# Feed-forward stages in turns of two batches, and later sends to the experts' slots, in a one-core transformer kernel

## The reference

```python
x = x + 0.5 * ffn(LN(x))       # 128 -> 512 -> 128, gelu, signs of w1 and a scale per row
x = x + gated_attention(LN(x)) # groups of 32 rows, a quadratic and a linear part
x = x + 0.5 * ffn(LN(x))       # the same weights once more
x = x + 0.5 * moe(LN(x))       # 8 experts, top 2, at most 76 rows per expert and batch, silu(h * g)
x = x + linear_attention(LN(x))# 16 heads, elu + 1
x = x + 0.5 * moe(LN(x))       # the same weights once more
```

## Time and profile before

| what | value |
|---|---|
| median of three runs | 2290.44 us (2286.01 to 2292.85) |
| profiled execution | 2287.4 us |
| its span on the core | 2285.4 us |
| mean granted TensorE clock | 0.987 of full |
| TensorE matmul busy | 2177.7 us, 95% |
| VectorE busy | 1520.7 us, 67% |
| ScalarE busy | 1241.2 us, 54% |
| GpSimd busy | 685.5 us, 30% |

### The profile page before, as it was taken

One profiled execution on the slowest core, in us unless ns is written; L12 is line 12 of the kernel. 1 busy time (PEld: TensorE's weight loads), 2 busy tenths in 40 slices (PEclk: granted clock), 3 DMA queues, 4 the chain that ended last, 5 costly groups with the idle time before them and its releaser, 6 DMA issues. The chain is left out here.

```text
span 2285.4 us, 42519 instructions
## 1 busy us (share of the span) xinstructions
PE 2177.7 (95%) x13706; PEld 1753.3 (77%) x13706; DVE 1520.7 (67%) x4922; ACT 1241.2 (54%) x2504; POOL 685.5 (30%) x724
## 2 busy tenths in 40 slices
PE   5989998999999999899999999999999899999995
PEld 5978888977777777777677777877777777777775
DVE  6867776866677776556666566666666676777664
ACT  4645445655444554465566665666665444544542
POOL 0412222433575555500000000000100344665545
PEclk9999999999999999999999999999999999999998
DMA  8040000000111111200000000000000011111222
GB/s 275 0 175 0 0 0 1 2 10 23 35 42 41 37 38 47 54 5 0 0 0 0 0 0 1 1 1 1 1 1 1 12 28 40 45 51 50 51 54 73
DMA packets 70648, 68.44 MB, mean 30 GB/s; under 512 B 9312, under 2 KB 57952, under 8 KB 70112
## 3 DMA queue, kind: packets, MB, share of 16 engines
q1 hardware_dynamic: 60960, 47.62, 6.5%
q0 software_dynamic: 8192, 16.79, 3.2%
q10 hardware_dynamic: 1344, 2.16, 0.3%
HBM read 32.47 MB, written 34.08 MB: 29 GB/s over the span
## 5 line engine op out<-in xcount | busy, mean ns | idle before, releaser
L2031 ACT ACTIVATE moe_fc<-moe_bank,all_b_fc 128x380 f32<-128x380 f32 (+2 forms) x448 | 245.8, 549 | 301.4 <-PE moe_bank L1961 298.3
L2138 DVE SCALAR_TENSOR_TENSOR moe_act<-moe_bank,all_b_moe_gate,moe_fc 128x380 f32<-128x380 f32 (+2 forms) x448 | 256.9, 576 | 169.5 <-PE moe_bank L1965 107.1
L1977 PEld LDWEIGHTS moe_bank<-all_w_proj,moe_act 128*128 128x128 f32 x2560 | 300.0, 192 | 12.2 <-issue 2.4
L1977 PE MATMUL moe_bank<-all_w_proj,moe_act 128*128 128x128 f32 x2560 | 305.7, 276 | 2.0 <-DVE moe_expert_out L2147 2.0
L1800 POOL DMA_INDIRECT all_landed<-rows_out,all_take_at x256 | 267.5, 1045 | 117.8 <-issue 114.5
L1494 POOL COPY lin_xn_ones<-lin_xn 128x254 f32<-128x254 f32 x32 | 12.7, 398 | 722.8 <-PE lin_bank L1244 722.4
L1876 POOL TENSOR_SCALAR moe_hot<-all_slot_ids,moe_slot 128x608 fp32r<-128x608 f32 x112 | 202.3, 1814 | 67.6 <-DVE moe_slot L2115 32.8
L2038 ACT ACTIVATE moe_act<-moe_act 128x760 f32<-128x760 f32 (+2 forms) x224 | 174.8, 780 | 85.0 <-DVE moe_act L2138 84.3
L1388 ACT ACTIVATE lin_neg<-lin_bank 128x512 f32<-128x512 f32 x256 | 151.7, 593 | 105.8 <-PE lin_bank L1236 62.1
L1286 PEld LDWEIGHTS lin_bank<-lin_kv,lin_qT 128*128 128x128 f32 x1024 | 145.1, 192 | 74.3 <-issue 62.3
L1961 PE MATMUL moe_bank<-gau_rowsT,all_w_fc 128*128 128x380 f32 (+2 forms) x448 | 171.4, 464 | 1.6 <-ACTq L2042 1.6
(11 more groups left out here) (248 smaller groups left out, 4557.0 us busy)
## 6 DMA issues: line engine op xcount, KB each, us to landing
rows_out<-moe_expert_out SPq DMA_DIRECT2D x96, 128.0 KB
rows_out<-all_zeros SPq DMA_DIRECT2D x1, 9728.0 KB, 28.8
rows_out<-moe_expert_out SPq DMA_DIRECT2D x80, 62.0 KB
all_landed<-rows_out,all_take_at POOLq DMA_INDIRECT x256, 2.8
out<-all_x SPq DMA_DIRECT2D x5, 640.0 KB, 4.5
all_w_fc<-in_w_fc SPq DMA_DIRECT2D x1, 2048.0 KB, 10.0
all_w_gate<-in_w_gate SPq DMA_DIRECT2D x1, 2048.0 KB, 13.9
all_w_proj<-in_w_proj SPq DMA_DIRECT2D x1, 2048.0 KB, 18.5
```

The lines of the kernel that those rows point to most:

```text
L1977: last = nc.tensor.matmul(bank[OUT][:, j * DIM:(j + 1) * DIM], act_in[:, i % 2, h, j * P:(j + 1) * P], k.w_proj[:, e * MC + h, :], start=( ...
L2031: nc.scalar.activation(fc[:, j, 0:c.width], bank[FC + j % 2][:, 0:c.width], ACT.Identity, bias=k.b_fc[:, e * MC + j:e * MC + j + 1]).then_ ...
L2138: nc.vector.scalar_tensor_tensor(act_in[:, i % 2, j, 0:c.width], bank[GATE + j % 2][:, 0:c.width], k.b_moe_gate[:, e * MC + j:e * MC + j + ...
```

## The change

In both feed-forward stages a turn takes two batches, so 16 turns of 512 columns. TensorE's turn p is now `transpose(p + 2)` (four), `up(p + 1)` (eight matmuls of 512 columns; the four PSUM banks of it are now one set, and each waits for its gelu of the turn before), `routing.on_tensor(2p)`, `down(p)` (32 records), `routing.on_tensor(2p + 1)`. ScalarE's turn is `high_part(p + 2)`, `gelu(p + 1)` (four of 512 columns), `routing.on_scalar(2p)`, `routing.on_scalar(2p + 1)`. VectorE's is `normalise(p + 3)`, `low_part(p + 2)`, `beside(2p)`, `add_out(p)`, `add_bias(p)`, `beside(2p + 1)`, where `beside` holds the pieces that stood behind a batch's turn. The normalised rows have one buffer in place of two. In the expert stages `slots_of` puts both sends one slot later, except for the last batch of each following chunk, and only where the step is five slots: four batches of five chunks in each of two stages.

```diff
             def _(pe):
...
-                def up(b, lag, par):
...
+                def up(p):
+                    pe.wait_ge(xT_sb.sem, xT_sb.at(p))
+                    for c in range(FC):
+                        if p:
+                            pe.wait_ge(h_sb.sem, h_sb.at(p - 1, 0, c))
+                        for j in range(2):
+                            last = nc.tensor.matmul(bank[c][:, :], k.w1T[:, c, :], parts[:, p % 2, j, :], start=(j == 0), stop=(j == 1))
                         last.then_inc(h_ps.sem, 1)
...
+                for p in range(TURNS):
+                    if p + 2 < TURNS:
+                        transpose(p + 2)
+                    if p + 1 < TURNS:
+                        up(p + 1)
                     if route:
-                        routing.on_tensor(pe, b)
+                        routing.on_tensor(pe, DUO * p)
+                    down(p)
+                    if route:
+                        routing.on_tensor(pe, DUO * p + 1)
...
+                for p in range(TURNS):
+                    if p + 2 < TURNS:
+                        high_part(p + 2)
+                    if p + 1 < TURNS:
+                        gelu(p + 1)
                     if route:
-                        routing.on_scalar(act, b)
-                    if b + 3 < BATCHES:
-                        high_part(b, 3, 1 - b % 2)
+                        routing.on_scalar(act, DUO * p)
+                        routing.on_scalar(act, DUO * p + 1)
...
+                for p in range(TURNS):
+                    if p + 3 < TURNS:
+                        normalise(p + 3)
+                    if p + 2 < TURNS:
+                        low_part(p + 2)
+                    beside(DUO * p)
+                    add_out(p)
+                    add_bias(p)
+                    beside(DUO * p + 1)
...
+SENDS = "send0", "send1"
...
-                for i, b in enumerate(plan[c.n + 1].batches):
+                follow = plan[c.n + 1].batches
+                for i, b in enumerate(follow):
+                    later = how.route_step[c.n] == 5 and b != follow[-1]
                     for what, lag in ROUTE_LAGS.items():
-                        work[i * how.route_step[c.n] + lag][what] = b
+                        work[i * how.route_step[c.n] + lag + (later and what in SENDS)][what] = b
```

More of the change, by code:

```diff
@@ L556, in ffn_stage, with rows @@
         last_row = k.sb("wv_last_row", [P, INNER]) if first else None
+        def rows(p):
+            return k.x[:, p * DT:(p + 1) * DT, :]
         with nc.Block() as block:
@@ L607, in add_out, with normalise @@
-                def add_out(b):
-                    dve.wait_ge(o_ps.sem, o_ps.at(b))
-                    if route:
[L610 to L615, removed]
+                def normalise(p):
+                    if p:
+                        dve.wait_ge(xT_ps.sem, xT_ps.at(p - 1))
+                    for t in range(DT):
+                        last = norm.apply(xn[:, t, :], 0, 0, p * DT + t)
+                    last.then_inc(xn_ready.sem, 1)
@@ L620, in add_bias @@
-                    for t in range(TILES):
-                        last = stats_of(k, b, t)
+                        dve.wait_ge(summed.sem, summed.at(p, 0, 1))
+                    for t in range(DT):
+                        last = nc.vector.bn_stats(k.stats[:, p * DT + t, :], k.x[:, p * DT + t, :])
                     last.then_inc(stat.sem, 1)
[L624 to L635, removed]
+                def own_norm(b):
+                    if first:
+                        if b < 4 or 8 <= b < 12:
+                            part = b // 8
+                            if b % 8 == 0:
+                                dve.wait_ge(k.x_in[KNOWN + part], 16)
+                            for t in range(2 * TILES):
+                                i = X_PART * (KNOWN + part) + 2 * TILES * (b % 8) + t
+                                last = nc.vector.bn_stats(k.stats[:, i, :], k.x[:, i, :])
+                            if b % 8 == 3:
+                                last.then_inc(late, 1)
+                                dve.wait_ge(late, 2 + part)
+                        elif b < 16:
+                            part, piece = b // 8, b % 8 - 4
+                            lo = X_PART * (KNOWN + part)
+                            norm.piece(dve, chain, lo, X_TILES if part else lo + X_PART, piece)
+                    elif b < PIECES:
+                        norm.piece(dve, chain, AHEAD, X_TILES, b)
@@ L636, in _, with beside @@
+                def beside(b):
+                    own_norm(b)
+                    next_norm(b)
+                    if route:
+                        routing.read_psum(dve, b)
+                        routing.on_vector(dve, b)
+                for p in range(2):
+                    normalise(p)
+                    low_part(p)
+                normalise(2)
                 if first:
@@ L639, in _ @@
                     dve.wait_ge(late, 1)
[L640 to L673, removed]
+                for p in range(TURNS):
[7 more added lines that the diff above has]
+                    beside(DUO * p + 1)
+                dve.wait_ge(stat.sem, stat.at(TURNS - 1))
                 if first:
@@ L715, in _ @@
[L715 to L728 removed]
+                transpose(0)
```

171 lines of the change are left out of this document (75 added, 96 removed).

## The result

The change makes the kernel slower: the ratio to the kernel before is 1.0035, 95% interval 1.0028 to 1.0041, which is 8.0 us (6.4 to 9.4). The medians of 20 runs each are 2297.73 us (2290.76 to 2300.21) after and 2288.77 us (2285.12 to 2292.85) before. The forecast was 1.9 us slower in a range of 2279 to 2304 us, so the direction and the range held and the size did not.

The account below looks back on a forecast made before the run. TensorE was taken to bound the feed-forward stages. ffn0 -5.6, ffn2 waits +8.4, clock +5.1 and sends -6.0 sum to +1.9 us on the 2290.4 us median: 2292.3 us, range 2279 to 2304.

Parts of the forecast that it names:

- The routing behind four wide gelus: ffn2, routers of turns 14 and 24, send1 of 16 and 26: TensorE waits 2.0 us each for ScalarE, 8.1 us.
- The last turn's send0: ffn2, turn 30: hot table ready about 3.4 us after down(14)'s sum, 0.9 passing anyway, so 2.5 us lost.
- send0 of turn 20: ffn2: it waits 1.3 us for a hot table VectorE makes behind sum, statistics and the choice of the turn before.
- the transposes did not wait at all: ffn2: two transposes of routed rows were forecast to wait some 0.3 us each.
- The clock: ffn2: two of the four 2.0 us waits and the 3.4 us one cost 1.7 us each, 5.1 us (0 to 17).
- Rival 3: ffn2: clock falls at each of five long waits, 1.7 to 3.4 us each; 2295.7 to 2304.2 us; chance 0.27.
- The wide turn: ffn0 and ffn2: a steady turn of two batches takes 5.74 us against 5.92, a gain of 0.18.
- The late start: ffn0: doubled norm, transposes, cast and low part, and up at half clock, delay the start 4.2 us (2 to 6).
- The streamed price: ffn0 and ffn2: at 131 ns per 512-column matmul, the stages would gain some 24 us more; forecast judged it unlikely.
- The sends: Expert stages: sends one slot later avoid waits for hot tables, 6 us gained (nothing to 12.6).
- the first batch wins nothing: Expert stages: a 0.4 us wait for normalised rows takes the place of the 0.47 lost to the hot table.
- hardly waits: Expert stages: the third batch's send hardly waits for its hot table; the fourth's little.

Follow-up runs that it names:

- the routing inside down: The change, with TensorE's even-turn routing in ffn2 placed behind three of down's four tiles instead of ahead of down; ratio 0.9953 to the kernel before, 10.8 us faster.
- the wide turns alone: The change with the sends left in their old slots; ratio 1.0045 to the kernel before, 10.3 us slower.
- the sends of two batches: The routing inside down, with later sends only for a chunk's second and fourth batch; ratio 0.9943 to the kernel before, 13.0 us faster.
- the copies between the gelus: The change, with ScalarE's even-turn routing copies in ffn2 between second and third gelu instead of behind the fourth; ratio 0.9989 to the kernel before, 2.5 us faster.
- the two buffers: The sends of two batches, plus two buffers for normalised rows in ffn0 and a reordered VectorE start; ratio 0.994 to the kernel before, 13.7 us faster.
- the later sends alone: The kernel before with only the expert stages' later sends, without wide turns; ratio 0.997 to the kernel before, 6.9 us faster.
- wide turns in ffn0 alone: The kernel before with wide turns only in ffn0, ffn2 and the sends as before; ratio 0.9969 to the kernel before, 7.1 us faster.

## Why the forecast held, and where its size came from

The mechanisms of the forecast were right, but for a loss in the expert stages that it put at nothing; several terms of its sum were mis-sized, most of them the same way. By stage it missed 1.4 us in ffn0, 4.7 in ffn2 and 4.0 in the expert stages, 10.1 us to the slow side. That the total missed by 6.1 only, and by 7.7 in the profiled execution, is luck: the gated attention, which the forecast did not name, gave 3.8 us back, 1.7 of them the clock at its start.

- **The routing behind four wide gelus.** Right in place, number and cause: priced at 2.0 us each, 1.74 to 2.03 measured. The last turn's send0 was priced at 2.5 beyond the time that passes anyway for the sum; it waits 3.22 us behind the same hot table, 2.44 more than the 0.78 us that the sum takes with the routing inside down. send0 of turn 20 took 0.55 us of the 1.3, and the transposes did not wait at all.
- **The clock**, the largest miss within ffn2: I charged two of the four waits and the last one, 5.1 us, and the clock fell at all five, 8.5 us. The unit price of 1.7 us from the earlier trace rows was right to 0.1; the count was not. (The 1.88 us there are all of the stretch's idle time; its one long wait is 1.81.) An idle time of 1.99 us that had cost nothing was no evidence for the next: here waits of 1.74 to 2.03 us cost the full price four times of four, and four of four again in the wide turns alone. Length alone does not decide it either: the wait of 2.27 to 2.30 us ahead of the first matmul of moe3 is followed by 10 us at 0.83 in four kernels (the change, the wide turns alone, the routing inside down, the sends of two batches) and by 10 us at 1.00 in two (the copies between the gelus, the two buffers). So a price per wait of this length is a likely one, and what decides stays open. Rival 3 is what happened in ffn2, with its place and its price at the lower end (1.7 us each); it said 2296 to 2304 us, and 2297.7 was measured, though other terms that were off have a part in that.
- **The wide turn.** The term "5.74 us against 5.92" was mis-sized: 5.88, so 0.04 us a turn and not 0.18, over fifteen turns of two stages some 4 us. I had doubled pieces read from start to start, and down of 16 records does not double: 1.71 to 3.57 us. Its records stand 0.112 us apart in both kernels (3.57 / 32), 16 of them 1.79 us; the 1.71 were short, since the up behind a narrow down starts before the last record is over. Behind the wide down stand the transposes, which lose by it: 0.36 us where 0.44 were priced. Up took 1.95 where 1.88 were priced, so 256 more columns cost 0.115 us a matmul and not 0.107. The late start went the other way: the first down after stood 2.3 us later (33.94 against 31.59) where I took 4.2; only the first wide up ran slow (3.76 us, the second 2.10; that the narrow one ran at half clock is read from its length alone, the granted clock of 24 to 28 us reads 1.00), and the wait of 1.10 us that the third transposes had before is gone. From the first down to the end of the last 90.8 us passed where 87.4 were forecast. Together: 4.2 us won, 5.6 forecast.
- **The streamed price.** By the 131 ns that the Trainium skill gives for a streamed matmul of 512 columns (page "TensorE: Matmul & The Clock Gate", section Back-to-back issue gap) up would take 1.05 us; it takes 1.95, 244 ns each, so the trace does not agree with that figure for these fp32r matmuls; the 216 ns of one alone is nearer.
- **The sends**, the other large miss: 6.0 us became 3 in the trace. The second batches gave what was forecast, 6.3 us in two stages for 5.9, and the fourth 1.3, put at little. That the first batch wins nothing was right from the third chunk on (0.40 lost for 0.47); in the first two chunks it loses, 0.7 us a stage, as the wait of 0.81 us for the second batch's hot table went and one of 0.92 for a norm, ahead of the first batch's send, came. That the third "hardly waits" missed that it can lose: its send had no wait to win, and now TensorE reaches the transposes ahead of it before their norm is done, 1.5 us a stage. These two losses, 4.4 us in two stages, were put at nothing, and the kernel with the second and fourth batch alone gives them back.
- **The gated attention** was not in the forecast: 1.5 to 2 us of it come with the wide turns in ffn0 in every trace, as the last section shows.

## What to carry to other kernels

When a turn is made wider, look for whatever stands between its pieces on one engine and waits for another engine's queue: the wider work in that queue now delays it, and a place behind a part of the work that does not depend on it (here three quarters of down) cost two waits of 0.8 us in place of 11 us of waits. For waits of nearly 2 us on TensorE reckon with the clock as well: here moving ScalarE's copies was worth 12 us in ffn2, of which the waits were 5, though not every wait of that length cost the clock. A step moved one slot wins only if what stands first in the later slot is not itself late: move it where the work ahead is long, and leave it where it is elsewhere.

## What the runs showed that was not expected

The gated attention is faster after a wide ffn0 in all seven kernels that have one, although no line of that stage differs: by 1.5 to 2.0 us in the four traces whose clock falls a second time at its start, as it does before, and by 3.7 to 4.3 in the three where it does not. VectorE's groups by line over 150 to 340 us show one place where the time may come from: the idle time "issue" ahead of its norm is 4.2 us before and 3.1 us after.

```profile
L262 DVE TENSOR_SCALAR gau_z<-all_x,all_mean,all_rstd 128x128 f32 (+1 forms) x56 | 17.3, 346 | 5.4 <-issue 4.2
```

```profile
L262 DVE TENSOR_SCALAR gau_z<-all_x,all_mean,all_rstd 128x128 f32 (+1 forms) x56 | 17.3, 346 | 3.6 <-issue 3.1
```

The first is the kernel before, the second the change; the later sends alone have the 4.2, wide turns in ffn0 alone the 3.1. That norm stands near the start of each pass of a loop, so the passes seem to restart sooner; that this is the cause, and why they should, was not tried. And the granted clock differs between executions of one kernel: at the start of the gated attention the stretch after its first idle time runs at 0.83 or at 1.00 in different kernels with the same code, 1.7 us apart, and what decides it stays open.
